# Experts in groups of four: slots laid out expert by expert, down products in four column groups, three bank pairs for the up products, and another deal of GpSimd's gathers and scatters

## What is computed

```python
logits = x @ wg.T
w_topk, idx_topk = top_k(softmax(logits), 8)
w_topk = w_topk / w_topk.sum(-1)
order = argsort(idx_topk.reshape(-1))            # rows sorted by expert
rank = position of a row within its expert       # rows with rank >= 160 are dropped
buf[expert, rank] = x[token]                     # 64 x 160 x 128
h = einsum("ech,efh->ecf", buf, expert_w1)       # 128 -> 2 x 384
x1, x2 = split(h, 2)
out = einsum("ecf,ehf->ech", x1 * silu(x2), expert_w2)   # 384 -> 128
combined = zeros.at[token].add(out[expert, rank] * w)
y = shared_out + combined
```

## Time and profile before

| | |
|---|---|
| median of three runs | 649.73 us (646.76 to 653.32) |
| profiled execution, span from first to last instruction | 688.8 us |
| mean granted TensorE clock | 0.959 |
| TensorE busy | 593.3 us (86%), 3947 matmul records |
| VectorE, ScalarE, GpSimd busy | 431.1, 247.9, 312.6 us |
| chain that ended last | TensorE 66%, VectorE 18%, "issue" 6% |
| DMA | 79.44 MB, mean 115 GB/s |
| first up product of the experts | 146.16 us |
| last scatter issued | 370.71 us |

### The profile page before, as it was taken

How to read it: one execution, slowest core, us unless ns; L and a number is a source line. 1 busy time by engine, 2 the same in 40 slices (tenths; PEclk the granted TensorE clock), 3 DMA queues, 4 the chain that set the end, 5 groups by cost and what they waited for, 6 DMA issues and landing times.

```text
span 688.8 us, 11455 instructions
## 1 busy us (share of the span) xinstructions
PE 593.3 (86%) x3947; PEld 493.7 (72%) x3947; DVE 431.1 (63%) x1330; ACT 247.9 (36%) x472; POOL 312.6 (45%) x313
## 2 busy tenths in 40 slices
PE   6999887669898897879879789799999999999881
PEld 5678655568898787879875767587777877787650
DVE  4588788953333234243433868687778777887793
ACT  3133254003222223222334034443444435444754
POOL 4765203876666666666552134322343223423431
PEclk9999998879999999999999989999999999999997
DMA  8970001227767667676715900000100000000001
GB/s 297 414 308 16 25 23 29 53 64 235 243 216 242 203 223 230 219 229 215 241 48 196 409 27 0 1 12 6 31 11 4 15 27 4 15 16 1 1 0 61
DMA packets 29565, 79.44 MB, mean 115 GB/s; under 512 B 7104, under 2 KB 12096, under 8 KB 29264
## 3 DMA queue, kind: packets, MB, share of 16 engines
q1 hardware_dynamic: 23088, 65.69, 27.1%
q0 software_dynamic: 6432, 13.16, 6.5%
HBM read 62.60 MB, written 16.25 MB: 114 GB/s over the span
## 4 chain that ended last, share of the span: by engine, by line
PE 66%; DVE 18%; issue 6%; another core or an unknown queue 3%; ACT 3%; POOL 1%; DMA 0%; DVEq 0%; ACTq 0%; SPq 0%; POOLq 0%
PE bank L799 12%; PE bank L980 8%; PE bank L968 8%; PE bank L809 7%; PE bank L903 4%; PE bank L559 4%; PE bank L924 3%; DVE arena L1756 2%; PE bank L878 2%; PE bank L894 2%; PE bank L944 2%; PE bank L915 2%; PE bank L591 2%; DVE hidden L1842 2%
## 5 line engine op out<-in xcount | busy, mean ns | idle before, releaser
L280 POOL TENSOR_TENSOR rstd<-veps,minus_half 128x4 f32<-128x4 f32 x52 | 54.0, 1038 | 231.2 <-DVE veps L273 225.7
L799 PE MATMUL bank<-hidden,ring 128*128 128x160 f32 x768 | 120.2, 307 | 3.3 <-DVE hidden L1830 2.5
L799 PEld LDWEIGHTS bank<-hidden,ring 128*128 128x128 f32 x768 | 111.0, 197 | 4.2 <-DVE hidden L1830 2.9
L1842 DVE TENSOR_TENSOR hidden<-bank,hidden 128x480 f32<-128x480 f32 x64 | 41.9, 654 | 113.8 <-ACT hidden L1227 64.8
L1460 POOL DMA_INDIRECT returned_rows<-x1t,scatter_all x80 | 79.8, 997 | 61.2 <-PE bank L799 26.0
L809 PE MATMUL bank<-hidden,ring 128*128 128x160 f32 x384 | 66.9, 311 | 28.6 <-DVE hidden L1842 21.4
L809 PEld LDWEIGHTS bank<-hidden,ring 128*128 128x128 f32 x384 | 56.5, 194 | 34.0 <-DVE hidden L1842 25.2
L1227 ACT ACTIVATE hidden<-bank 128x480 f32<-128x480 f32 x64 | 37.3, 582 | 107.3 <-PE bank L799 65.3
L1453 POOL DMA_INDIRECT arena<-dispatch_rows,gather_all x50 | 53.1, 1063 | 33.2 <-DVE scatter_all L1788 14.1
L1292 ACT ACTIVATE arena<-bank,layer_cols 128x512 f32<-128x512 f32 x64 | 43.9, 687 | 60.7 <-PE bank L968 60.7
L980 PE MATMUL bank<-ring,arena 128*128 128x128 f32 x512 | 59.9, 275 | 1.4 <-issue 1.4
(11 more groups left out here) (231 smaller groups left out, 1097.3 us busy)
## 6 DMA issues: line engine op xcount, KB each, us to landing
ring<-in_ew SPq DMA_DIRECT2D x64, 576.0 KB
returned_rows<-zeros SPq DMA_DIRECT2D x16, 512.0 KB, 15.6
arena<-returned_rows SPq DMA_DIRECT2D x6, 512.0 KB, 13.4
hidden<-returned_rows SPq DMA_DIRECT2D x4, 512.0 KB
ring<-returned_rows SPq DMA_DIRECT2D x4, 512.0 KB
ring<-in_l1w SPq DMA_DIRECT2D x8, 256.0 KB, 2.6
returned_rows<-x1t,scatter_all POOLq DMA_INDIRECT x80
shared<-in_xr SPq DMA_DIRECT2D x1, 1024.0 KB, 8.0
```

Source lines behind the costliest of these rows:

```text
L280: pool.tensor_tensor(rstd[:, s, :], veps[:, s, :], minus_half[:], ALU.pow).then_inc(sem(f"rstd{which}_ready"), 1)
L799: mm = pe.matmul(bank[2 * (n % 2) + part][:, CAP * f:CAP * f + CAP], ring[:, n % RING, P * (FB * part + f):P * (FB * part + f) + P], E["xt ...
L1842: v.tensor_tensor(E["prod"][:, n % 2, :], bank[2 * (n % 2)][:, 0:FB * CAP], E["silu"][:, n % 2, :], ALU.mult).then_inc(sem("prod_g_ready"), 1)
```

## The change

Partition p of a group's tile now holds slot 32 b + p % 32 of expert p // 32, so an expert owns 32 partitions. The slot search computes only what is needed: four matmuls of 10 columns, each with 32 columns of weights, into the four quarters of the partitions. The down product takes the hidden values as weights (32 slots at a time) and w2 as the moving data, four experts into the four quarters, so that its output already stands by slots: the transposes of results and ScalarE's copies fall away. Silu and product share one buffer for 8 experts in the arena; the up products rotate over three bank pairs; down products of group Q - 1 stand at the third and fourth expert of group Q.

Parts of the diff; left out are constants, buffers that only move, and waits that are renamed. In `turn_inputs` an `xt_read` wait is added for groups 1 and 2, and `turn_results` is gone.

```diff
-        GOT, BACK = 8, 3
+        GOT, BACK = 8, 4
...
+        PROD = 2 * EG
+        E = carve([("prod", (PROD, FB * CAP), F32)], TILES * RA * EG // 2 * EG)
+        E.update(carve([("back", (BACK, RB, D), F32)], NEG * TILES * RA * EG // 2))
+        E["xt"] = flat_hidden[:, 0:2 * EG * CAP].rearrange("p (u e s) -> p u e s", u=2, e=EG)
...
-        LAG = 2
         FIRST, REST = range(0, 3), range(3, RB)
+        HIDDEN = 3
...
+            def load_up(n):
+                sp.dma_start(ring[:, n % RING, 0:2 * FFN], ew[n][:, 0:2 * FFN]).then_inc(
+                    sem(f"expert_then_tile_in{n % RING}"), 16)
+
+            def load_down(Q):
+                at = EG * Q % RING
+                sp.dma_start(ring[:, at:at + EG, 2 * FFN:], ew[EG * Q:EG * Q + EG].rearrange("n p c -> p n c")[:, :, 2 * FFN:]
+                             ).then_inc(sem(f"down_in{Q % 2}"), 16)
...
             for n in range(RING, NE):
-                sp.wait_ge(sem("expert_mm"), n - RING + LAG + 1)
-                sp.dma_start(ring[:, n % RING, :], ew[n]).then_inc(sem(f"expert_then_tile_in{n % RING}"), 16)
-
-            sp.wait_ge(sem("rows_mm"), NE + LAG - 1)
+                sp.wait_ge(sem("expert_mm"), n - RING + 1)
+                load_up(n)
+                if n % EG == 2 and n // EG >= 3:
+                    sp.wait_ge(sem("result_mm"), 2 * (n // EG - 2))
+                    load_down(n // EG - 1)
+            sp.wait_ge(sem("result_mm"), 2 * (NEG - 2))
+            load_down(NEG - 1)
+
+            sp.wait_ge(sem("result_mm"), 2 * (NEG - 1))
...
                 for k, q in enumerate(FOUND[call]):
                     pe.wait_ge(sem("one_hots_ready"), 2 * q + 2)
                     for u in range(2):
-                        at = 2 * RB * EG * (2 * k + u)
-                        lo = EG * (2 * q + u)
+                        Q, at = 2 * q + u, 2 * RB * (2 * k + u)
                         for i in range(TILES):
-                            mm = pe.matmul(slot_bank(call)[:, at:at + 2 * RB * EG], a16[:, 2 * q + u, i, :],
-                                           b16[:, :, i, lo:lo + EG], start=(i == 0), stop=(i == TILES - 1))
+                            for e in range(EG):
+                                mm = pe.matmul(slot_bank(call)[RA * e:RA * e + RA, at:at + 2 * RB], a16[:, Q, i, :, e],
+                                               b16[:, :, i, EG * Q + e], start=(i == 0), stop=(i == TILES - 1))
                 mm.then_inc(sem("slots_mm"), 1)
...
             def expert_hidden(n):
+                Q, j = n // EG, n % EG
+                if j == 0:
+                    pe.wait_ge(sem("xt_read"), 2 * (Q + 1))
+                if n >= HIDDEN:
+                    pe.wait_ge(sem("prod_g_ready"), n - HIDDEN + 1)
+                pe.wait_ge(sem(f"expert_then_tile_in{n % RING}"), 16 * (n // RING + 1))
                 for part in (1, 0):
                     for f in range(FB):
-                        mm = pe.matmul(bank[2 * (n % 2) + part][:, CAP * f:CAP * f + CAP],
+                        mm = pe.matmul(bank[2 * (n % HIDDEN) + part][:, CAP * f:CAP * f + CAP],
                                        ring[:, n % RING, P * (FB * part + f):P * (FB * part + f) + P],
-                                       E["xt"][:, n // EG % 2, n % EG, :], start=True, stop=True)
-                return mm
-
-            def expert_result(n):
-                pe.wait_ge(sem("prod_g_ready"), n + 1)
-                if n >= 2:
-                    pe.wait_ge(sem("yt_ready"), n - 1)
-                for f in range(FB):
-                    mm = pe.matmul(bank[4 + n % 2][:, 0:CAP], ring[:, n % RING, P * (2 * FB + f):P * (2 * FB + f) + P],
-                                   E["prod"][:, n % 2, CAP * f:CAP * f + CAP], start=(f == 0), stop=(f == FB - 1))
-                return mm
+                                       E["xt"][:, Q % 2, j, :], start=True, stop=True)
+                mm.then_inc(sem("expert_mm"), 1)
+
+            def expert_results(Q, c):
+                if c == 0:
+                    pe.wait_ge(sem("prod_g_ready"), EG * (Q + 1))
+                    pe.wait_ge(sem(f"down_in{Q % 2}"), 16 * (Q // 2 + 1))
+                if Q + 2 < NEG:
+                    pe.wait_ge(sem("xt_read"), 2 * (Q + 2) + c + 1)
+                else:
+                    pe.wait_ge(sem("back_read"), 2 * (Q - 1) + c + 1)
+                for k, b in enumerate(REST if c else FIRST):
+                    for f in range(FB):
+                        for e in range(EG):
+                            n = EG * Q + e
+                            mm = pe.matmul(bank[6 if c else 7][RA * e:RA * e + RA, P * k:P * k + P],
+                                           E["prod"][:, n % PROD, CAP * f + RA * b:CAP * f + RA * b + RA],
+                                           ring[:, n % RING, P * (2 * FB + f):P * (2 * FB + f) + P],
+                                           start=(f == 0), stop=(f == FB - 1))
+                mm.then_inc(sem("result_mm"), 1)
...
             for n in range(NE):
                 Q, j = n // EG, n % EG
-                if n >= LAG:
-                    done = expert_result(n - LAG)
-                if j == 0 and Q >= 2:
-                    done = turn_results(Q - 2, 1)
-                elif Q == NEG - 1 and j >= 2:
-                    done = turn_results(Q - 1, j - 2)
-                elif j in (1, 2) and Q < NEG - 1:
-                    done = turn_inputs(Q + 1, j - 1)
-                elif j == 3 and Q >= 1:
-                    done = turn_results(Q - 1, 0)
-                if n:
-                    done.then_inc(sem("rows_mm"), 1)
-                if j == 0:
-                    pe.wait_ge(sem("xt_read"), 2 * (Q + 1))
-                pe.wait_ge(sem(f"expert_then_tile_in{n % RING}"), 16 * (n // RING + 1))
-                expert_hidden(n).then_inc(sem("expert_mm"), 1)
-            expert_result(NE - 2).then_inc(sem("rows_mm"), 1)
-            expert_result(NE - 1).then_inc(sem("rows_mm"), 1)
+                if j < 2 and Q + 1 < NEG:
+                    turn_inputs(Q + 1, j)
+                elif j >= 2 and Q >= 1:
+                    expert_results(Q - 1, j - 2)
+                expert_hidden(n)
             for c in range(2):
-                turn_results(NEG - 1, c).then_inc(sem("last_turned"), 1)
+                expert_results(NEG - 1, c)
...
+            for n in range(NE):
+                act.wait_ge(sem("expert_mm"), n + 1)
+                act.activation(E["prod"][:, n % PROD, :], bank[2 * (n % HIDDEN) + 1][:, 0:FB * CAP], ACT.Silu).then_inc(
                     sem("silu_ready"), 1)
...
-            BEFORE, FIRST_SCATTER = 4, 2 * EG
-
-            def gather_blocks(first, count):
-                for k in range(first, min(first + count, NEG * RB)):
-                    gather_block(k // RB, k % RB)
-
             pool.wait_ge(sem("rows_out"), 16 * 2 * GROUPS)
-            gather_blocks(0, BEFORE * RB)
+            for Q in range(GOT):
+                for b in range(RB):
+                    gather_block(Q, b)
             pool.wait_ge(sem("zeroed"), 16 * TOK * TOPK // (8 * P))
-            PACED = FIRST_SCATTER + 12 * EG
-            for n in range(PACED):
-                pool.wait_ge(sem("expert_mm"), n + 1)
-                if n < FIRST_SCATTER:
-                    gather_blocks(BEFORE * RB + 2 * n, 2)
-                else:
-                    Q = (n - FIRST_SCATTER) // EG
-                    gathering = BEFORE * RB + FIRST_SCATTER + n < NEG * RB
-                    for b in (((0,), (1,), (2, 3), (4,)) if gathering else ((0, 1), (2, 3), (4,), ()))[n % EG]:
-                        scatter_block(Q, b)
-                    gather_blocks(BEFORE * RB + FIRST_SCATTER + n, 1)
-            for Q in range((PACED - FIRST_SCATTER) // EG, NEG):
+            gathers_by = lambda s: min((4 * s + 3) // 5, RB * (NEG - GOT))
+            for Q in range(NEG):
                 for b in range(RB):
+                    pool.wait_ge(sem("expert_mm"), min(EG * (Q + 1) + 2 + EG * b // RB, NE))
                     scatter_block(Q, b)
+                    for m in range(gathers_by(RB * Q + b), gathers_by(RB * Q + b + 1)):
+                        gather_block(GOT + m // RB, m % RB)
...
                 v.wait_ge(sem("slots_mm"), call + 1)
-                v.tensor_tensor(picked[:, 0:n], slot_bank(call)[:, 0:2 * RB * EG * n].rearrange(
-                    "p (u b e) -> p u b e", u=n, e=EG), own.unsqueeze(1).unsqueeze(1).to_broadcast([P, n, 2 * RB, EG]),
-                    ALU.mult).then_inc(sem("slots_read"), 1)
-                v.wait_ge(sem("slots_read"), call + 1)
-                ch.after(ch.did(v.tensor_reduce(slots[:, qs].rearrange("p g t b -> p g (t b)"), picked[:, 0:n], AX.X,
-                                                ALU.add)))
-                tok1, place1 = slots[:, qs, 0, :], slots[:, qs, 1, :]
+                found = slot_bank(call)[:, 0:2 * RB * n].rearrange("p (u t b) -> p u t b", u=n, t=2)
```

(18 more changed lines are left out.)

89 lines of the change are left out of this document (26 added, 63 removed).

## The result

The changed kernel takes 660.38 us (median of four, 659.40 to 661.25); the kernel before took 651.53 us beside it (four runs, 646.76 to 653.57). The ratio is 1.016, 95% interval 1.012 to 1.020: slower by 1.6%, where 645 us and a small gain were forecast. The profiled execution's own time is 660.33 us with a span of 658.0, so this time profile and median can be compared directly.

What follows compares the result with a forecast made beforehand. In ordinary runs TensorE and GpSimd were taken to bound the expert stage together, ending within 2 us of each other. 649.7 us less 3 for the stage's end and 2 for pauses gave 645 us, range 638 to 652, chance 0.5.

Steps and rivals of the forecast that it cites:

- Ordinary runs hardly have the pauses: Expert stage: the 28.6 us idle before down products belongs to the profiled execution; the rival, real in every run, chance 0.2.
- The 2 us that I gave the change for the rest of the pauses: Expert stage: later down products and three bank pairs save 2 us of whatever pauses ordinary runs have.
- A group of 10.96 us, four column groups overlapping whole: TensorE, expert stage: four experts take 10.96 us, with down products at 3.5 us plus 0.4 us for entries.
- The slower rivals: Down matmuls overlap only three at once (5.1 us a group, 666 us) or two (7.4 us, 703 us); chance 0.1 each.
- the proportion worked out from the Trainium skill: Down products: four tiles overlap only 3.2 times, 4.8 us a group, 14 us in all, 661 us.
- 3 us less for the stage's end: Expert stage: TensorE's path and GpSimd's DMAs both end at 329 us where now it is 332.
- GpSimd without idle time to 329 us: Expert stage: GpSimd issues its gathers and scatters without waiting from 149 to 329 us.
- the cover of the pauses: Up products: waiting on the product of three experts back covers pauses of 1 to 2.6 us, up to 28.6 us when profiled.
- The failed step: Slot search ahead of the expert stage: 1024 small matmuls delay the first experts by 1 us, first gather unchanged.
- the lower end: Slot search: the 1024 matmuls cost what the 256 do, 0.97 us for 32 and 3.76 us for 128.
- The upper end: Slot search: each small matmul costs as much as one now, 768 x 0.029 = 22.6 us, ending at 155.4 instead of 142.5.
- The third rival: The slot search becomes the wait: at 0.029 us a matmul experts start 12 us later, 658 us; chance 0.1.

Runs made afterwards that it cites:

- the kernel with both: The changed kernel with 256 search matmuls (weight step of 8 bytes) and the first eight experts loaded whole: 652.84 us, ratio 1.0035 to the kernel before.
- the deal: How GpSimd's gathers and scatters are ordered; dealt as in the kernel before, tried on the kernel with both: 660.37 us, 7.5 us more.
- 2048 matmuls: The changed kernel with every table's search matmuls issued twice, 2048 small ones instead of 1024: 687.05 us, ratio 1.056 to the kernel before.
- the probe: The kernel before with four stretches of idle matmuls (768, 512, 512, 256) behind its last result; 128 small ones took 3.66 us.
- the four copies: The kernel before with 128, 512, 1024 and 2048 idle matmuls behind its end; first search matmuls at 110.11, 111.77, 112.90 and 113.51 us.

## Why the prediction was wrong, point by point

*Ordinary runs hardly have the pauses:* right. The fetch in an ordinary run was put at 334 us, it came at 332.99. The 2 us that I gave the change for the rest of the pauses were not there: 0.5 us is all there was to win.

*A group of 10.96 us, four column groups overlapping whole:* right, 11.01 us. The slower rivals (5.1 and 7.4 us a down part) are out. So is the proportion worked out from the Trainium skill, "TensorE: Matmul & The Clock Gate", Part 3 (2.38 for three column tiles), an estimate of 4.8 us: the trace has 3.55, or 3.95 if what the group takes beyond up products and transposes is counted (11.01 - 4 x 1.63 - 0.54).

*3 us less for the stage's end, 4 us for its length* (experts 1 us later, end 3 us earlier): right in direction, 2.6 us measured. From first up product to fetch it was 332.99 - 144.34 = 188.7 us, and is 343.67 - 157.60 = 186.1 us, 185.6 in the kernel with both. One of its terms was wrong. The forecast let only two scatters follow the last gating instead of five. In the traces of both kernels GpSimd waits last for the gating of the last group's first tiles, and five scatters follow (to 330.71 in the kernel before, to 341.34 in the changed one):

```profile
325.53 1.01 POOL L1460 DMA_INDIRECT returned_rows<-x1t,scatter_all  x1 [1.60 <-DVE x1t L1853]
```
```profile
336.16 0.98 POOL L1444 DMA_INDIRECT returned_rows<-arena,scatter_all  x1 [1.37 <-DVE arena L1825]
```

What was gained lies ahead of them: 325.53 - 144.34 = 181.2 us against 336.16 - 157.60 = 178.6 us. Which part of the change gained it was not tried by itself.

*GpSimd without idle time to 329 us:* in the changed kernel it runs free to 313 us and then waits for TensorE, which started late. What the deal is worth the prediction did not ask: 7.5 us beside the new lag of the down products. The third bank pair, which it took for the cover of the pauses, covers nothing in an ordinary run.

***The failed step is the slot search.*** "I take a value near the lower end [...]: first experts 1 us later." The lower end came from 256 matmuls at 0.97 us for 32, and nothing in the trace spoke of what the code of 1024 matmuls costs to bring in. Measured: 43.5 - 34.3 = 9.2 us later by the search. The upper end, every matmul as dear as before (0.029 us each), had nearly the right price for another reason: the matmuls do overlap, at 12 ns, but their code comes at 28.6 ns each. It put 22.6 us on the last 768; they took 155.19 - 135.24 = 20.0 us, as the first 167 ran without a pause. The third rival had the place, but its time (658 us) is near the measured one by luck: its 12 us for the search were 9.2, and the 4.0 us of the late start were not in it. I gave it 0.1 because two tiles beside each other had lost nothing. That argued about the array, where the limit was ahead of it.

*Not in the prediction at all:* the start, 4.0 us later (114.11 - 110.07). Together +4.0 + 9.2 - 2.6 = 10.6 us at the fetch (343.67 against 332.99 is 10.7), and 1.5 us less behind it: 658.0 - 648.8 = 9.2 us of span, against 8.9 us between the medians. With 256 search matmuls the same sum is +2.7 + 1.0 - 3.1 + 0.7 = 1.3 us, 650.1 - 648.8. That the search is the cause of most of the loss is shown: with 256 matmuls 6.6 to 7.6 us go (653.80 against 660.38, 652.84 against 660.44) of the 8.9 between the medians, or 10.5 against the 649.85 us of the 29 later runs of the kernel before. That a longer program starts late is shown as a relation over twenty profiles, not as a mechanism.

## What to carry to other kernels

Splitting a matmul into smaller ones on column groups keeps the array's time but multiplies the instructions: before trusting the overlap, compare the stretch with 3.66 us for each 256 instructions on TensorE (3.85 beside other traffic, in the changed kernel); the sign of a stretch below that pace is idle time on "issue" at regular counts. The split costs nothing where the stretch around it is slower than the code (a group of experts, 173 records in 11.01 us, 64 ns each, no pauses), and it costs 9 us where the small matmuls stand alone. Neighbours in the queue belong on different column groups. Where a profiled execution is far longer than the runs, profile again before reasoning from its pauses.

## What the runs showed of the hardware

- Code for TensorE: 128 matmuls with their weight loads in 3.66 us, 28.6 ns each, with the rest of the core idle; pauses of 2.3 to 2.8 us at each block. With other traffic 3.85 us (changed kernel) and (185.28 - 146.41) / 10 = 3.89 us (2048 matmuls). One 16 KB packet of code for each 128 matmuls, in the probe and the four copies. From a standing start the first pause of the probe comes after 152 matmuls.
- Four 32-column tiles in turn: 1.19 us for 128 matmuls of 10 columns, 9.3 ns each. Full-width matmuls of 10 columns take 7.01 / 256 = 27 ns. Three in a row on one tile: 6.0 against 3.55 us for 60 of the down products.
- Half-precision weights whose 128 columns lie 32 bytes apart: 66 ns a matmul of 40 columns (12.60 us for 192); 8 bytes apart 35 ns (4.46 us for 128). The mean granted clock was 0.76 and 0.92 in the two stretches, which explains a part of it at most. On two column groups of 64 it is 4.04 against 2.14 us for 64 matmuls at 0.88 and 1.00, and 61 against 32 ns in the long stretches at 0.56 and 0.61, so the distance makes most of it.
- In the 15 profiles with a TensorE program longer by 1024 matmul records or more TensorE waits 1.8 to 3.5 us at about 9 us, mostly for an input load, where the other five have 0 to 1.4, and the search starts at 112.31 us or later instead of by 111.77. The cause is open.
